# A GNN kernel on one core: GpSimd fills 768 idle columns behind every fourth gather, from group 16 on

## The reference

```python
# layer 0: weighted messages
msg = relu((x[src] * edge_weight[:, None]) @ W_msg + b_msg)
agg = segment_sum(msg, dst)
x = layernorm(x + relu(agg @ W_out + b_out))
# layers 1 and 2: one of 8 relation matrices per edge
xt  = einsum('nd,rde->rne', h, W)           # a table of 8 x 12500 rows
h   = relu(segment_sum(xt[edge_type, src], dst) + h @ SW + b)
# after layer 2
x = layernorm(x + h)
```

## Time and profile before

| what | value |
|---|---|
| time, median of 3 runs (lowest, highest) | 6096.66 us (6094.32, 6098.1) |
| span of the profiled execution, first to last instruction | 7175.4 us |
| mean granted TensorE clock in it | 0.633 of full speed |
| GpSimd busy | 4562.2 us (64%), 4,835 instructions |
| VectorE busy | 2671.7 us (37%) |
| TensorE matmul busy, weight load busy | 2668.5 us (37%), 2091.2 us (29%) |
| ScalarE busy | 606.3 us (8%) |

### The profile page before, as it was taken

How to read it: one execution, slowest core, us unless ns; L and a number is a source line. 1 busy time by engine, 2 the same in 40 slices (tenths; PEclk the granted TensorE clock), 3 DMA queues, 4 the chain that set the end, 5 groups by cost and what they waited for, 6 DMA issues and landing times.

```text
span 7175.4 us, 45352 instructions
## 1 busy us (share of the span) xinstructions
PE 2668.5 (37%) x11892; PEld 2091.2 (29%) x11892; DVE 2671.7 (37%) x5892; ACT 606.3 (8%) x1334; POOL 4562.2 (64%) x4835
## 2 busy tenths in 40 slices
PE   4334344433444343444444444443223223222223
PEld 4333333322333322223332333332222222222222
DVE  3776666666555532333332222232111111111112
ACT  2111111111111110000000000000000000000000
POOL 4666666666666646666666666665666666666665
PEclk9666666666666656666666666665555555555556
DMA  5122222222222212222222222221111111111111
GB/s 144 43 78 74 71 73 72 73 74 71 73 74 72 74 55 61 70 68 70 69 69 69 68 67 67 69 70 57 52 52 52 52 53 51 52 52 51 52 51 49
DMA packets 265749, 468.98 MB, mean 65 GB/s; under 512 B 102461, under 2 KB 155365, under 8 KB 265477
## 3 DMA queue, kind: packets, MB, share of 16 engines
q0 software_dynamic: 154112, 315.93, 17.0%
q1 hardware_dynamic: 110212, 149.64, 6.1%
q10 hardware_dynamic: 1152, 0.39, 0.0%
HBM read 343.56 MB, written 122.05 MB: 65 GB/s over the span
## 4 chain that ended last, share of the span: by engine, by line
another core or an unknown queue 48%; DVE 22%; issue 17%; PE 10%; DVEq 2%; ACT 1%; DMA 0%; SPq 0%; POOL 0%; ACTq 0%; POOLq 0%
PE bank L791 6%; DVE rows L769 5%; PE bank L1031 3%; DVE picked L1070 2%; DVE work L751 2%; DVE place L1081 2%; DVE onehot L751 2%; DVE tab L1091 1%; DVEq L776 1%; DVE agg L781 1%; DVE bank L1385 1%; DVE work L1386 1%; DVE bank L1383 1%; DVE work L1390 1%
## 5 line engine op out<-in xcount | busy, mean ns | idle before, releaser
L688 POOL DMA_INDIRECT rows<-rel_table,rel_index x3152 | 2980.9, 946 | 1643.4 <-issue 939.0
L688 POOL DMA_INDIRECT rows<-msg_table,msg_index x1600 | 1514.0, 946 | 918.9 <-issue 466.9
L791 PE MATMUL bank<-work,rows 128*128 128x128 f32 x6304 | 1188.1, 336 | 1300.7 <-issue 1282.2
L781 DVE TENSOR_TENSOR agg<-agg,bank 128x128 f32 x602 | 171.2, 284 | 3803.2 <-remote 3486.7
L791 PEld LDWEIGHTS bank<-work,rows 128*128 128x128 f32 x6304 | 1084.7, 249 | 1438.0 <-issue 1419.9
L791 PE MATMUL bank<-onehot,rows 128*128 128x128 f32 x3328 | 624.5, 361 | 890.6 <-ACT rows L657 498.8
L791 PEld LDWEIGHTS bank<-onehot,rows 128*128 128x128 f32 x3328 | 583.4, 268 | 960.3 <-ACT rows L657 524.1
L1031 PE MATMUL bank<-wr,feat 128*128 128x512 f32 x784 | 598.5, 907 | 693.1 <-issue 429.7
L751 DVE TENSOR_TENSOR work<-bank,place 128x1024 f32<-128x1024 f32 x394 | 477.1, 1212 | 7.3 <-ACT agg L956 3.8
L1031 PEld LDWEIGHTS bank<-wr,feat 128*128 128x128 f32 x784 | 207.2, 293 | 898.8 <-issue 619.6
L1020 PE MATMUL bank<-ident,sums 128*128 128x128 f32 x98 | 38.1, 389 | 1055.3 <-ACT sums L994 842.8
(11 more groups left out here) (126 smaller groups left out, 1437.0 us busy)
## 6 DMA issues: line engine op xcount, KB each, us to landing
rel_table<-tab SPq DMA_DIRECT2D x196, 512.0 KB
rows<-rel_table,rel_index POOLq DMA_INDIRECT x3152
rows<-msg_table,msg_index POOLq DMA_INDIRECT x1600
x_dram<-normed SPq DMA_DIRECT2D x98, 64.0 KB
xin<-x_dram SPq DMA_DIRECT2D x98, 64.0 KB
xin<-in_x_dram SPq DMA_DIRECT2D x97, 64.0 KB
out_dram<-normed SPq DMA_DIRECT2D x97, 64.0 KB
tab<-in_x_dram SPq DMA_DIRECT2D x24, 256.0 KB
```

What stands on the lines that cost most here:

```text
L688: nc.gpsimd.indirect_dma_start(rows[:, u, t, :], None, table, bass.IndirectOffsetOnAxis(ap=table_index[:, g, t:t + 1], axis=0)).then_inc(e ...
L781: nc.vector.tensor_tensor(out=window, in0=window, in1=sum_of(layer, st), op=ALU.add).then_inc(sems.added, 1)
L791: ins = nc.tensor.matmul(total, tile, hot[:, t, :], start=t == 0, stop=t == TPG - 1)
```

## The change

Behind gather 3 and gather 7 of each group GpSimd gets one fill with zeros of 128 partitions by 768 columns of float32. In layer 0 it writes the first columns of `work` and begins with group 16; in layers 1 and 2 it writes six of the eight tiles of `onehot`, for every group. Nobody reads what it writes. Each fill waits for the semaphore of the fill before it. Two waits are new where buffers change hands before layer 1: GpSimd waits until all groups of layer 0 have been added, and VectorE until all fills of layer 0 are done.

```diff
+        s_rest = sem("s_rest")
...
+        REST = 6 * P
+        FIRST_REST = 2 * EARLY
+        idle = [work[:, 0:REST]] + [onehot[:, 0, 0:REST // P, :]] * 2
+        rests = [0]
+
+        def pool_rest(layer):
+
+            need(nc.gpsimd, s_rest, rests[0])
+            nc.gpsimd.memset(idle[layer], 0.0).then_inc(s_rest, 1)
+            rests[0] += 1
+
         def static_gather(layer, g):
...
                     bass.IndirectOffsetOnAxis(ap=table_index[:, g, t:t + 1], axis=0)
                 ).then_inc(edge_main.rows[u][t // HALF], 16)
+                if t % HALF == HALF - 1 and (layer or g >= FIRST_REST):
+                    pool_rest(layer)
...
                     if layer == 1 and trim:
+                        eng.wait_ge(edge_main.added, COUNT[0])
                         eng.wait_ge(s_unpacked, len(TURNS))
                 if eng is nc.vector and layer:
                     eng.wait_ge(node_sems[layer - 1].agg, BLOCKS)
+                if eng is nc.vector and layer == 1 and trim:
+                    eng.wait_ge(s_rest, 2 * (COUNT[0] - FIRST_REST))
```

## The result

The change takes the kernel from 6097.38 to 6818.73 us (medians of four runs each); the ratio is 1.118, 95% interval 1.117 to 1.120. The forecast was 6,887, the range 6,640 to 7,130. It took 6,097 us in the runs above, 6,097 and 6,099 us on chips 13 and 8 (the lower level from here on), and 7,131, 7,172 and 7,135 us on chips 10, 9 and 0 (the upper level). No numbered chip showed both, but the runs of a chip were taken together, so that the level belongs to the chip is likely and not shown. The profile of before ahead of the prediction (7175.4 us) is of the upper level, the times beside it are of the lower; on which chip it was taken isn't known.

What follows compares the result with a forecast made beforehand. GpSimd's own stream, 4,816 gathers at about 1.25 us, was taken to set the end. 1,169 counting fills at 0.676 us add 790 us to 6096.66, giving 6,887 us, 13% slower; range 6,640 to 7,130.

Steps and rivals of the forecast that it cites:

- unprofiled, the gathers run at 1.22 to 1.25 us almost without a break: GpSimd's 4,816 gathers in the timed runs: their stream sets the end, without the profile's 949 us of waits.
- That profiling itself causes this is my inference, from the two totals: GpSimd's 949 us of waits for TensorE: put down to profiling, from the 7,175 us span against the timed 6096.66.
- under the profiler the fills can vanish in the waits, and the profiled span after may be 7,150 to 7,400: Profiled groups take 11.4 to 11.85 us, with two fills 11.35 needed; timed runs would still grow by 790 us.
- the fills vanish in waits in the timed runs too: Rival at the wait for the group eight back: 6,097 us, no slower; chance 0.05 for absorbing waits, 0.04 wholly.
- The price of a fill: GpSimd, fill of 768 columns: 0.14 + 640 x 0.84 ns = 0.676 us, next gather's gap kept; 1,169 count, 790 us.
- the rival of the covering gap: The 0.30 us gap before the next gather covers part of the fill: 0.38 to 0.60 us each, 6,536 to 6,798; chance 0.15.
- The record: Pricing fills by reported duration, 0.732 us, instead of start-to-start spacing: 856 us in place of 790.
- The switching cost: Rival: switching between fill and gather costs, 0.80 to 1.20 us a fill, 7,032 to 7,500; chance 0.14.
- The semaphore waits and the new waits at layer 1: Each fill's wait for the fill before, and GpSimd's and VectorE's new waits before layer 1: all priced at nothing.
- the number of partitions doesn't matter: Fill price on GpSimd: depends on columns only, read from long fills on 8 partitions and short ones on 128.
- The lock with VectorE: VectorE's 196 normalising rows might each hold up one GpSimd fill by 0.35 us: 68 us more, 790 to 858.
- Start, boundaries and tail: Time of the profiled span outside the gathers and the waits for the group eight back: 206 us.

Runs made afterwards that it cites:

- half_rows: Kernel before, every second gather from group 16 on fetching 64 rows instead of 128, no fills; lower level both times, 6027.16 against 6097.49 us, ratio 0.989.
- half_matmuls: Kernel before without half of TensorE's edge products from group 16 on, no fills; 6097.30 against 6097.49 us on chip 13, 7084.34 against 7134.54 on chip 0.
- after_again: The changed kernel, unchanged, on another chip beside before; 7124.44 against 7172.48 us, ratio 0.993.
- the other widths: Changed kernel with fills of 1, 384 and 1024 columns in place of 768; 7138.22, 7113.78 and 7161.86 us against 7131.02 of before.
- fill_1: Changed kernel with fills of 1 column in place of 768, all semaphores kept; 7138.22 against 7131.02 us of before, ratio 1.001.

## Why the prediction was right, and where its reasons weren't

**What bounds the kernel**: GpSimd's stream at 1.25 us a gather, shown for the lower level (half_rows, half_matmuls, and the sum of the profile after). The prediction's step "unprofiled, the gathers run at 1.22 to 1.25 us almost without a break" holds at its upper end.

**The profile of before**: the step that doesn't stand is "That profiling itself causes this is my inference, from the two totals". The two totals were of two levels of the same kernel; recorded executions reach the lower one as well. Whether recording has a part in the upper one is open. From the inference followed "under the profiler the fills can vanish in the waits, and the profiled span after may be 7,150 to 7,400": the span was 6,814.6, as the timed runs. The arithmetic of that sentence wasn't idle, though. It comes near to the upper level: 11.22 us a group is less than 11.4 to 11.85, and after_again took 7,124. That is luck, since the forecast tied the range to profiling and not to a level.

**The rival "the fills vanish in waits in the timed runs too"** got 0.05, on the condition that a gather takes 1.05 us. The condition was wrong, since it took waits of the upper level and the 6,097 of the lower one for the same execution; where such waits exist before takes 7,131, the gather still 1.25. At the upper level that rival is what happens: on chip 9 for the changed kernel itself, on chip 10 for the other widths, whose times lie within 0.5% of before. On chip 0 no version with fills was run. That the forecast met the result therefore depended on both kernels being timed at the lower level, which the prediction took for granted.

**The price of a fill**: 0.676 forecast, 0.612 by the step, 721 / 1,169 = 0.617 by the times. Of the two terms, the column price was right (0.84 ns). What was mis-sized is the fixed part: the forecast had 0.03 on top of the columns' 0.64, and it is 0.03 below them, since the gap before the next gather shrinks from 0.30 to 0.17 and the fill starts without one (0.757 + 0.165 - 0.004 - 0.30 = 0.62, 0.01 above the median step by rounding). So the rival of the covering gap was right in kind for 0.13 of the 0.30. It gives 6,536 for the whole gap and had its place from 0.60 down; 0.612 is within the forecast's own 0.60 to 0.80. The record, 0.757, by which the sum would be 856, is further off than the spacing: the Trainium skill (Perfetto Trace Analysis, GPSIMD Engine Instruction) advises the spacing, and the trace agrees.

**The switching cost** of 0.17 at the first gather isn't there: fill_1 has a step of 1.249. The semaphore waits and the new waits at layer 1 cost nothing in the changed kernel (fill_1; 2330.69 to 2360.05 is covered by the table's wait of 28.60); where two fills stand together 0.14 is paid, perhaps for the wait. That the number of partitions doesn't matter didn't follow from the prediction's rows, where it changed together with the columns; the later widths, all on 128 partitions, have the same 0.84 ns.

**The lock with VectorE**, up to 68 us, was put on the wrong side. No fill is held up: 83 fills overlap a normalising row, and the steps across them are 1.857 to 1.871, as elsewhere. But VectorE is held up. In the view of the normalising line (1117 in the changed kernel) the longest row is 1,608 ns, where it was 561:

```profile
L1117 DVE TENSOR_SCALAR normed<-y,mv,rstd x196: 345/348/1608, 251.8 to 6811.1; 128x128 f32<-128x128 f32 x196
```

```profile
740.98 0.94 POOL L700 DMA_INDIRECT rows<-msg_table,msg_index  x1 [0.30 <-issue]
...
741.39 1.37 DVE L1117 TENSOR_SCALAR normed<-y,mv,rstd 128x128 f32<-128x128 f32 x1
...
741.92 0.76 POOL L687 MEMSET work<- 128x768 f32 x1
```

The row starts beside a gather, would need 0.35 us, and ends 0.08 us after the fill that follows the gather. All 81 rows that overlap a fill and last over 0.6 us end 0.081 to 0.085 us after the fill's end, and the 196 rows take 75 us more than at 348 ns each. So the two engines do exclude each other here, and it is VectorE that waits. It costs nothing that can be seen in the time here, where VectorE doesn't set the end; what it costs in a kernel that VectorE bounds no run here shows. Start, boundaries and tail, 206 us in the profile of before, are 77 at the lower level, waits included (6,097 less 6,020); they cancelled in the difference.

## What to carry to other kernels

When a profile's span and the timed median of the same kernel differ by far more than runs differ, neither blame the profiler nor clear it from the totals: look for the profiled execution's own time, and profile again. Here the two numbers were of two levels of the same kernel, and the price of an edit was 12% on the one and -0.7% on the other. An engine's idle gap before each instruction of one kind may hide the fixed part of another kind put there, but not its columns; a one-column version of the edit shows that in one trace, whatever the total does. When an edit adds work to one engine, look at the longest rows of the others too, and not at medians alone: the median of VectorE's row stayed at 348 ns while over 80 of 196 were held up.

## What was unexpected of the hardware

Two levels of one kernel on different chips, 6,097 and 7,131 to 7,172 us, each steady within 0.5%, with equal gather records (943 to 947 ns). The mean granted TensorE clock of before was 0.64 at the lower and 0.63 at the upper. At the upper one TensorE's signals end VectorE's waits 14 us late in the median and up to 50, and the lateness vanishes when fills of 1024 columns bring a group only every 11.68 us. Halving TensorE's products moved that level by 0.7%, a queue of three groups in place of eight by 0.2%. Its traces hold 20,000 to 70,000 semaphore updates where the lower level has about 100,000; the cause of both isn't known. No version here beats before by more than 0.7% at the upper level, and none that computes the same result beats it at the lower.

A fill of GpSimd that follows a gather without a break holds up a VectorE row of 0.35 us that starts beside the gather, until 0.08 us after the fill's end; the row then lasts up to 1.6 us (trace of after; 0.56 at most in that of before).
